# A two-layer network in four stages, rewritten as one program per engine with its last three stages woven batch by batch

## The reference

```python
x = L0_attn_hidden_states                                  # (4, 512, 256), fp32
x = _layernorm(x + _L0_attn_ref(x, ...), axis=-1)          # 16 heads, causal softmax, rope
x = _layernorm(x + _L0_ffn_ref(x, ...), axis=-1)           # the "wave" sublayer
x = _layernorm(x + _L1_attn_ref(x, ...), axis=-1)          # linear attention, elu+1 features
x = _layernorm(x + _L1_ffn_ref(x, ...), axis=-1)           # six blocks 256 -> 1024 -> 256, gelu
```

## Time and profile before

| | us |
|---|---|
| median of 3 runs (1192.38 to 1195.21) | 1192.47 |
| the profiled execution | 1189.87 |
| its span, first to last instruction | 1188.1 |
| PE busy in the span | 1048.0 (88%) |
| DVE busy | 774.8 (65%) |
| ACT busy | 618.6 (52%) |
| POOL busy | 297.8 (25%) |

### The profile page before, as it was taken

The page is one execution under the profiler, slowest core; times in us unless marked ns, Lnnn a source line. Parts: engine busy times, 40 slices in busy tenths (PEclk is TensorE's granted clock), DMA queues, the critical chain, the costliest instruction groups (busy, mean ns, idle before and its releaser), DMA issues. The chain is left out here.

```text
span 1188.1 us, 20755 instructions
## 1 busy us (share of the span) xinstructions
PE 1048.0 (88%) x6653; PEld 868.3 (73%) x6653; DVE 774.8 (65%) x2207; ACT 618.6 (52%) x1186; POOL 297.8 (25%) x417
## 2 busy tenths in 40 slices
PE   6888998999885598277879999999999999999995
PEld 5455555556575588166768899899989998998895
DVE  5566775776535888844784676767567657766754
ACT  4456555563456354452245654665466456645650
POOL 3344353451204201100120142123222321331200
PEclk9588997998997798579979999999999999999998
DMA  6000010030101000010121011011000010110111
GB/s 217 20 1 20 6 34 1 18 108 33 40 9 71 1 0 0 1 74 1 37 71 37 1 37 36 2 36 35 0 35 28 7 35 0 35 35 1 37 36 36
DMA packets 29165, 36.57 MB, mean 31 GB/s; under 512 B 1732, under 2 KB 26536, under 8 KB 29096
## 3 DMA queue, kind: packets, MB, share of 16 engines
q1 hardware_dynamic: 24552, 31.02, 7.8%
q10 hardware_dynamic: 4544, 4.72, 1.3%
HBM read 31.40 MB, written 4.20 MB: 30 GB/s over the span
## 5 line engine op out<-in xcount | busy, mean ns | idle before, releaser
L2093 ACT ACTIVATE G<-ps,bias_col 128x512 f32<-128x512 f32 x192 | 135.2, 704 | 188.1 <-PE ps L2011 177.5
L2026 PE MATMUL ps<-w_h,G_h 128*128 128x256 f32 x768 | 217.7, 283 | 1.4 <-DVE rsum L2154 1.4
L2026 PE MATMUL ps<-w_h,G_l 128*128 128x256 f32 x768 | 217.3, 283 | 0.0
L2026 PE MATMUL ps<-w_l,G_h 128*128 128x256 f32 x768 | 217.1, 283 | 0.0
L2145 DVE TENSOR_TENSOR G_l<-G,G_h 128x512 fp32r<-128x512 f32 x192 | 144.8, 763 | 62.6 <-ACT G_h L2094 62.4
L1973 POOL TENSOR_TENSOR x_a<-xn,mlp_g 128x1024 f32<-128x1024 f32 x20 | 70.2, 3509 | 369.3 <-DVE xn L2177 369.3
L668 ACT ACTIVATE probs<-ps 128x512 f32<-128x512 f32 (+3 forms) x256 | 98.2, 438 | 119.6 <-PE ps L810 119.2
L1069 DVE CUSTOM_DVE_ANT_0 ps<-ps,q_mask 128x128 f32<-128x128 f32 (+3 forms) x256 | 121.4, 511 | 53.8 <-PE ps L799 49.5
L2011 PE MATMUL ps<-xT_h,w_h 128*128 128x512 f32 x384 | 153.7, 400 | 1.7 <-PEq L1622 1.7
L2011 PE MATMUL ps<-xT_l,w_h 128*128 128x512 f32 x384 | 152.3, 397 | 0.0
L2011 PE MATMUL ps<-xT_h,w_l 128*128 128x512 f32 x384 | 152.2, 396 | 0.0
(11 more groups left out here) (283 smaller groups left out, 2144.6 us busy)
## 6 DMA issues: line engine op xcount, KB each, us to landing
w_raw<-L_ffn_W_T SPq DMA_DIRECT2D x12, 1024.0 KB, 5.1
hs<-L_attn_hidden_states SPq DMA_DIRECT2D x8, 512.0 KB, 3.5
x_kept<-hs SPq DMA_DIRECT2D x4, 512.0 KB, 2.9
w_raw<-x_kept SPq DMA_DIRECT2D x2, 1024.0 KB, 5.5
out<-xn SPq DMA_DIRECT2D x4, 512.0 KB, 2.9
w_raw<-L_ffn_ent_w_T SPq DMA_DIRECT2D x1, 1024.0 KB, 10.1
w_raw<-L_ffn_ent_pw SPq DMA_DIRECT2D x1, 1024.0 KB, 12.3
heads_T<-neg_rows SPq DMA_DIRECT2D x64, 2.0 KB
```

The source lines that it names most:

```text
L2026: mm = pe.matmul(ps[:, 4 + t // 2, (t % 2) * D:(t % 2 + 1) * D], x[:, b % 2, f, t * P:(t + 1) * P], w[:, f, :], start=(k == 0), stop=(k == ...
L2093: act.activation(G32[:, n % 4, :], ps[:, n % 4, :], ACT.Gelu, bias=bias)
```

## The change

The two middle entries of `attention0` and the first three maps' turns are written out instead of looped (the loop over the feed-forward's blocks stays). All four functions share one block, so no engine waits for all others between stages; each first use of a tile or a bank waits for its own semaphore. `wave_ffn`, `attention1` and `ffn1` become one function `rest`, with all tiles at places that are chosen by hand. In the parts that were loops, the carriers are gone and the waits sit on the instructions.

```diff
-            with eng.Fori(1, B - 1) as i:
+        for i in range(1, B - 1):
                 entry(i, "loop")
-                    v.sem_inc(g.carrier["v_carrier"], 1)
                     v.tensor_tensor_reduce(
...
-                pool.tensor_copy(g.x_a[:, bass.ts(b, RT), :], xn[:, 0, :, :]).then_inc(s["g_x1"], 1)
+            pool.tensor_tensor(g.x_a[:, b * RT:(b + 1) * RT, :], xn[:, 0, :, :], bcast(g.last_b, 1, [P, RT, D]), ALU.add
+                               ).then_inc(s["g_x1"], 1)
```

The gates use three banks instead of two. ACT computes batch 0's angles among the gates of batches 0 to 2; the Square goes to DVE as `-2 x x`, and so does `gated_low`:

```diff
+        act.wait_ge(s["v_split"], STAGES)
+        half_angle(act, g, 0)
+        whole_angle(act, g, 0)
+        for n in range(4, 10):
+            gate_function(act, g, n)
...
-                pool.tensor_tensor(g.xT_l[:, b, :, :], amp[:, b, :, :], g.xT_h[:, b, :, :].bitcast(F32),
-                                   ALU.subtract).then_inc(s["g_xl"], 1)
+def gated_low(v, g, b):
+    v.wait_ge(g.wave["a_hh"], b + 1)
+    v.tensor_tensor(g.xT_l[:, b, :, :], g.amp[:, b, :, :], g.xT_h[:, b, :, :].bitcast(F32), ALU.subtract
...
+        square(v, g, chain, 1)
+        gated_low(v, g, 0)
+        gated(v, g, chain, 1)
+        square(v, g, chain, 2)
+        gated_low(v, g, 1)
+        gated(v, g, chain, 2)
+        moments(0, 0)
```

The splitting of the second attention's weights, which stood between gates, moves into the maps, and the product with `last_g` to DVE. The end of the wave is put ahead of and between the first units:

```diff
+            if st == 0:
+                act.wait_ge(first["l1_in"], 64)
+                act.activation(g.wq_h, raw_l1[:, 0, :, :], ACT.Copy).then_inc(wave["a_l1"], 1)
...
+            if st == 1:
+                v.wait_ge(wave["a_l1"], 3)
+                v.tensor_tensor(g.wq_l, raw_l1[:, 0, :, :], g.wq_h.bitcast(F32), ALU.subtract)
...
+            chain.step(v.tensor_tensor(sums(b), normed(b), bcast(last_g, 1, [P, RT, D]), ALU.mult))
+            yield
...
+        run(sum_up(0))
+        moments(END, B - 1)
+        run(sum_up(1))
+        low(END, 0)
+        run(sum_up(2))
+        low(END, 1)
+        steps = sum_up(3)
```

PE's program at the end of the second attention, where the hidden tiles of the feed-forward's first two batches now stand between its steps. ACT normalises (`normalise_next`) where DVE did:

```diff
+        transpose_attention(2)
+        hidden(0, 0, (0, 1))
+        key_values(3)
+        hidden(0, 0, (2, 3))
+        project(2)
+        for half in range(2):
+            numerators(3, half)
+            transpose_next(1, half)
+        hidden(0, 0, (4, 5, 6, 7))
+        transpose_attention(3)
+        hidden(0, 1, (0, 1, 2))
+        project(3)
+        transpose_next(2, 0)
+        hidden(0, 1, (3,))
+        transpose_next(2, 1)
+        hidden(0, 1, (4, 5, 6, 7))
```

More of the change, by code:

```diff
@@ L241 @@
+        g.small = place(top, nc, "small", 20 * D - 16)
+        g.last_b = put(nc, "last_b", g.small, 20 * D - 16 - D, [D])
+        attention0(nc, A, g, top)
+        rest(nc, A, g, out)
 J_ORDER = (0, 3, 1, 2)
@@ new lines, in _ @@
+        pe.wait_ge(first["v_tail"], 3 * KC)
+        for n in range(4 * (B - 1), 4 * B):
+            gate_product(pe, g, n)
+        pe.wait_ge(wave["g_zero"], 3)
+        pe.wait_ge(wave["v_c"], 1)
+        pe.wait_ge(first["v_split"], STAGES)
+        linear(0, 0)
+        linear(0, 1)
+        pe.wait_ge(first["a_gate"], 4 * B)
+        linear(0, 2)
+        for st in range(END):
+            for b, (later, done) in TURN:
+                turn(st, b, normed(b), wave["a_norm"], st * B + b + 1)
+                linear(st + later, done)
```

3308 lines of the change are left out of this document (1676 added, 1632 removed).

## The result

The changed kernel took 1159.70 us (median of 4 runs, 1155.65 to 1162.98) against 1193.84 us before (median of 4 runs, 1192.38 to 1195.60): a ratio of 0.9707 with a 95% interval of 0.9683 to 0.9732, 34 us faster. The forecast was 1168.9 with a range of 1155 to 1182. The profiled execution of the changed kernel took 1162.98 us, the longest of its four, so the profiles differ by 26.9 us only.

What follows compares the result with a forecast made beforehand. PE was taken to bound the feed-forward, DVE helped by ACT the stretch behind the maps. Terms -2.6 - 15.8 + 4.0 - 6.7 - 2.5 = -23.6 us gave 1166.3 profiled, 1168.9 for the median, range 1155 to 1182.

Steps and rivals of the forecast that it cites:

- First attention, -2.6: First attention: carriers gone -3.6, loop's turn gone -1.7, longer `keep` +2.7; sum -2.6 us, bounds -9.5 and +5.
- the carriers: First attention: removing semaphore-step instructions ahead of others saves 0.12 us at 30 waits of PE, 3.6 us; bounds 0 and 7.0.
- `keep`: First attention: POOL's copy of 1.04 us becomes a sum of 2.39, charged at two heads of entries, +2.7 us.
- Front of the wave, -15.8: Attention's tail to the maps' first `low`: new queues bring that `low` from 406.05 to 390.2, 15.8 us earlier.
- port waits: Head of the maps: four small DVE instructions wait until POOL's sums end, costing 8 us before the change.
- The maps, +4.0: Maps' turns: weight copies and differences now delay DVE's `low`, +3.2 us at the second turn's head, +0.8 at the next.
- Closing norm and first units, -6.7: After the maps: overlapped norms and units end 18.5 us earlier in all; less the front and maps, -6.7 for this part.
- The weave, -2.5: Second attention's step 4 to first output: overlap alone saves 15 us, two queue stands leave -2.5; bounds -10 and +4.
- code that arrives late: Rival: straight-code entries and turns are fetched anew; 12 stalls of 2.54 us make it 1199 us; slower, chance 0.04.
- no move at all: Rival: first-use semaphores release at the same instants as the walls between functions, so time stays 1192 us; chance 0.03.
- a tail that gives nothing: Rival: of the wave's tail only port waits (8) and walls (6.0) pay, maps' +4.0 stays: 1182.5 us; chance 0.24.
- full pay: Rival: carriers give -7.0 instead of -3.6 and the weave -10 instead of -2.5: 1157.9 us; chance 0.19.

Runs made afterwards that it cites:

- pool_sums_late: Changed kernel with POOL's `keep` a plain copy and its four `last_b` sums waiting for the wave's first linear product: 1161.97 us, 0.9737 of the kernel before.
- tail_order: Changed kernel with three orders exchanged at the closing norm, on ACT, DVE and PE: 1157.64 us, 0.9695 of the kernel before.
- l1_early: Changed kernel with ACT's four weight copies moved between the last two gates and DVE's four differences ahead of the first moments: 1149.75 us, 0.9629 of before.
- Weave_order: Changed kernel with ACT's norm of batch 2 behind Gelu 6 and DVE's weight differences and low part reordered in the weave: 1144.55 us, 0.9583 of before.

## Why the prediction was right, and where it was wrong

**First attention, -2.6: mis-sized, some 6 us too small.** The mark says -1.9 and -9.7 in the two profiles, and -4.5 in the mean of the six with this code, against a profiled execution of before (1189.87) that is itself 2 to 4 us faster than that kernel's medians (1191.66 to 1194.14). The medians tell more: of their 33.9 to 34.1 us, 25.0 to 25.9 lie behind the last norm, and 8 to 9 remain for the attention. This is an estimate from the two spans, and takes before to be as steady behind that norm as the other kernels are. The mechanisms are there, the sizes are not: the carriers were to give 3.6 and give 9 by medians, good to 5; the loop was to give 1.7 and gives 5.2 (7.4 in one trace); `keep` was to cost 2.7 and costs 4.9 in the mean of straight profiles and 5.6 in the looped code. The step that failed is the price of a wait. 0.12 us times 30 counts what PE waits, and that came out right (3.7 more in the one profile). What it leaves out is that the products beside the waits run longer, in entry 0 by 2.6 us for 1.0 us of waits. The prediction charged the cold clock in the weave, where it saw stands, and not in the attention, where they are many and small. Its own sign, an attention that ends more than 5 us earlier, came true. By luck the profiled execution had its entry 0 at 0.77 and its gates at 0.90, which hid 5.3 and 1.95 us against the second profile and made the term look right.

**Front of the wave, -15.8: right** in size (-15.6 and -16.1). The 8 us of port waits are shown as a mechanism by pool_sums_late, with 5 to 6 where they were rebuilt; the same sums 7 us earlier cost 1. The rest of the term, the first wall, the third bank and the new order of gates, angles, squares and low parts, was not tested piece by piece; it rests on the walk, which came out within 0.3 us by the last norm and 0.4 to 2.1 by the first gate. In the rows of tail_order a table load takes 1.28 us and the exponential begins 0.02 later, as the sum had it. The drain of 1.38 us that the Trainium skill (ScalarE: Activation LUTs, What ACT_TABLE_LOAD costs) adds is not seen there either.

**The maps, +4.0: right** (+4.2, +4.0), and l1_early takes back 4.0. The head of turn 2 reads as it was walked: DVE waits 3.56 for the last copy and begins `low` at 414.26. By turns it is +2.9 and +1.3 in the first profile where +3.2 and +0.8 were said.

**Closing norm and first units, -6.7: 4.0 short.** DVE's part was right: `low` of batches 0 and 1 wait 2.6 each as foretold. From the end of the low of batch 1 on, 22.1 us were allowed and 18.4 were needed: counted from there the sums of batch 3 were done 1.5 earlier than walked, PE's later transposes took 1.18 and 1.09 (warm), not 1.97, and the remaining half microsecond is not assigned. That the norm's order holds the units was only half right: with it changed, 1.1 us came back, since ACT's queue has the exponentials behind the same norm. No run takes the overlap itself away, so the 10.7 us are read from the two traces and not rebuilt.

**Second attention up to step 4: +1.5 where 0 was said.** Its code is unchanged. In the first profile PE waits as long in this stretch (8.99 against 8.89 us) and is busy for 40.46 instead of 38.89 us, at a clock of 0.93 instead of 0.96; a cause for that was not tried.

**The weave, -2.5: right** (-2.7), with both stands where they were walked: 4.53 us behind ACT's norm of batch 2 and 5.11 behind DVE's queue. Weave_order shows that order alone makes them. The bound of -10 was too near: without them the stretch is 14.6 us shorter than before, since the clock stays at 1.00.

**Feed-forward, 0: 1.9 off.** Every second output product is a little shorter, 11.37 us from its first product to the next stage (727.18 to 738.55) against 11.50 before (752.54 to 764.04); the other half takes 11.5 to 11.6 in both. Twelve such give 1.6. The tiles of `G` of even batches lie at other places than before and so do those of odd ones, and only the even ones gained. It is the same in all thirteen profiles with the new places, 540.4 to 540.6 us for the stage. Which property of the place it is was not tried.

**Sum.** The forecast was the median before less 23.6 us, and the medians differ by 34.1. Of the missing 10.5 us some 6 are the attention's, 4.0 the closing norm's and 1.9 the feed-forward's, and the second attention took 1.5 to 1.7 back. What the three walls cost by themselves stays open, since no run puts one back. Of the other rivals, code that arrives late is out (no straight version has such a stall), and so is no move at all; a tail that gives nothing is out by the 10.7 us of the closing norm. The time lies outside the 1162 to 1176 that were given the best chance; the range held because full pay (1157.9) was among the rivals. The time is nearer to it than to the forecast, though for it the prediction had the weave pay in full, and it was the attention and the closing norm that did. That part is luck.

## What to carry to other kernels

Where PE stops and starts, a wait costs more than its length, since the products beside it can fall to the low clock: taking two stands of 9.6 us out of the weave gave 11.9, and in entry 0 of the attention 1.0 us of waits came with 2.6 us of slower products. It is no fixed rate: over the whole attention six profiles of one code differ by 9.4 us in PE's busy time, and the one with the fewest waits is among the busiest (27.9 and 261.6). When stages are woven, walk each engine's queue and look for an instruction that waits for something late with ready work behind it: exchanging two such orders gave more than any other edit here. And find out how far one stage differs between profiles of the same code before you set two profiles against each other; where one stage is unsteady and the rest is not, the medians less the steady rest give its size.

## What the runs showed of the hardware

- The same code ran entry 0 of the attention in 64.4 to 64.8 us at a clock of 0.85 in nine profiles and in 69.6 to 69.7 in two (0.77 in the one shown), with PE waiting as long (7.59 and 7.40 us). Which of the two an execution gets was not found. With carriers it was 68.1 to 68.3 us at 0.82 in three profiles, with 8.5 to 8.7 us of waits.
- With a POOL copy of 1.04 us for a sum of 2.4 in `keep`, the attention from entry 1 to the first gate took 216.9 to 217.6 us in five profiles, with the sum 219.3 to 225.0 in six.
- DVE instructions of 128x4 that met a POOL sum of 1024 columns ended with that sum, after 2.25 to 2.27 us instead of 0.16. One of 128x1024 took 3.29 us for 1.23 and ended 1.1 us behind the first sum; the sum after that took 3.38 us where the last two took 2.4. `BATCH_NORM_AGGREGATE` was not held up beside it (359.90, 0.15 us, while POOL's sum ran).
- The second turn of the loop over the attention's middle entries began with 2.54 and 2.76 us in which DVE waited for nothing that the profile shows. The other loops (the maps before, the feed-forward in all kernels) had no such stall above 1 us, nor had any straight version.
